# FFN weights freed of their mean, the first quad's q and k laid out by TensorE, the last y loaded in two parts, and new slots: a causal attention and FFN kernel on one core

## What is computed

```
def ffn(x):        # base + correction, W is 256x256, V_r and C have rank 32
    return x @ W.T + b + (x @ V_r) @ C.T

x = x + 0.5 * ffn(layernorm(x))          # "ln1"
q, k, v = split(layernorm(x) @ W_attn)   # "ln2"
s = q @ k.T / 4, causal
a = (s*s + 1 if s > 0 else 1 - s/100) / 1000
x = x + (a @ v) @ W_proj
x = x + 0.5 * ffn(layernorm(x))          # "ln3"
```

## Time and profile before

| | us |
|---|---|
| median of 3 runs | 1777.77 (1775.73 to 1783.82) |
| the profiled execution | 1776.91 |
| its span | 1775.2 |
| PE busy | 1620.3 (91%) |
| ACT, DVE, POOL busy | 1379.9, 1349.2, 1292.4 |
| first score starts at | 55.4 |
| last product of the attention ends at | 1734.45 |
| mean granted TensorE clock | 0.976 |

### The profile page before, as it was taken

How to read it: one execution, slowest core, us unless ns; L and a number is a source line. 1 busy time by engine, 2 the same in 40 slices (tenths; PEclk the granted TensorE clock), 3 DMA queues, 4 the chain that set the end, 5 groups by cost and what they waited for, 6 DMA issues and landing times.

```text
span 1775.2 us, 67710 instructions
## 1 busy us (share of the span) xinstructions
PE 1620.3 (91%) x27158; PEld 822.4 (46%) x27158; DVE 1349.2 (76%) x3229; ACT 1379.9 (78%) x2214; POOL 1292.4 (73%) x1455
## 2 busy tenths in 40 slices
PE   6787989999998999999998999999998999899994
PEld 3453444444445544444445544444455545344442
DVE  4767777878787787878887787887878677788881
ACT  2456768988887888888886888888887887788881
POOL 2566657777878896878878797877878787677662
PEclk9888999999999999999999999999999999999997
DMA  3653532432446443332436534243434535322211
GB/s 100 182 161 102 167 117 81 131 90 79 116 115 175 136 145 112 112 112 80 145 100 167 167 114 136 80 132 103 130 104 141 156 99 157 90 69 67 81 41 53
DMA packets 183222, 206.16 MB, mean 116 GB/s; under 512 B 27004, under 2 KB 156916, under 8 KB 181116
## 3 DMA queue, kind: packets, MB, share of 16 engines
q1 hardware_dynamic: 182908, 201.77, 39.2%
HBM read 123.65 MB, written 76.30 MB: 113 GB/s over the span
## 4 chain that ended last, share of the span: by engine, by line
PE 60%; DVE 15%; POOL 9%; ACT 8%; issue 5%; DMA 1%; SPq 1%; POOLq 0%; ACTq 0%; DVEq 0%
PE y_ps L1215 23%; PE score L1215 18%; PE bank L1215 16%; DVE rp L1148 9%; POOL rp L938 4%; ACT rp L1045 3%; PE bank L1241 3%; ACT rp L1065 2%; DVE lin L1154 2%; POOL z L900 2%; DVE bnst_ln L1173 1%; POOL rp L913 1%; PE bank L1280 1%; POOL lin L913 1%; ACT rp L1061 1%
## 5 line engine op out<-in xcount | busy, mean ns | idle before, releaser
L1148 DVE TENSOR_SCALAR rp<-score 128x512 f32<-128x512 f32 (+3 forms) x1728 | 973.1, 591 | 274.4 <-PE score L1215 272.5
L938 POOL TENSOR_TENSOR rp<-rp 128x1024 f32<-128x1024 f32 (+3 forms) x416 | 710.9, 1716 | 95.1 <-DVE rp L1148 82.5
L1215 PE MATMUL score<-qs,ks 96*32 96x512 bf16 (+3 forms) x10240 | 722.0, 352 | 51.8 <-DVE lin L1154 21.7
L1215 PE MATMUL y_ps<-rp,vt 128*16 128x512 f32 (+3 forms) x5120 | 599.5, 536 | 36.2 <-DVE lin L1154 12.2
L1045 ACT ACTIVATE rp<-score 128x512 f32<-128x512 f32 (+3 forms) x832 | 435.4, 561 | 203.8 <-PE score L1215 199.3
L1215 PEld LDWEIGHTS score<-qs,ks 96*32 96x32 bf16 x10240 | 299.1, 96 | 431.6 <-DVE rp L1148 161.2
L1061 ACT ACTIVATE rp<-rp,rise 128x1024 f32<-128x1024 f32 (+3 forms) x416 | 438.8, 1077 | 6.5 <-POOL rp L913 6.4
L913 POOL TENSOR_SCALAR_AFFINE_SELECT rp<-rp 128x256 f32<-128x256 f32 (+1 forms) x400 | 189.9, 475 | 262.0 <-ACT rp L1045 191.7
L1065 ACT ACTIVATE rp<-rp 128x2048 f32<-128x2048 f32 (+2 forms) x224 | 342.6, 1529 | 16.0 <-POOL rp L913 14.6
L1154 DVE SCALAR_TENSOR_TENSOR lin<-score,slope_mask 128x128 f32<-128x128 f32 x736 | 206.3, 280 | 0.0
L1215 PEld LDWEIGHTS y_ps<-rp,vt 128*16 128x16 f32 x5120 | 138.0, 96 | 133.6 <-issue 32.4
(11 more groups left out here) (80 smaller groups left out, 1293.6 us busy)
## 6 DMA issues: line engine op xcount, KB each, us to landing
ks<-part_scratch SPq DMA_DIRECT2D x648, 64.0 KB, 2.4
qs<-part_scratch SPq DMA_DIRECT2D x384, 64.0 KB, 2.3
part_scratch<-parts SPq DMA_DIRECT2D x14, 1536.0 KB, 5.9
vt<-v_scratch SPq DMA_DIRECT2D x103, 128.0 KB, 2.6
state_scratch<-st_new SPq DMA_DIRECT2D x16, 528.0 KB
x_sb<-in_L_attn_x_dram SPq DMA_DIRECT2D x16, 512.0 KB, 4.4
x_scratch<-x SPq DMA_DIRECT2D x16, 512.0 KB, 5.4
qT_scratch<-qkT SPq DMA_DIRECT2D x16, 512.0 KB, 3.3
```

The lines of the kernel that those rows point to most:

```text
L938: pool.tensor_tensor(half, half, half, ALU.mult).then_inc(squared["pool"], 1)
L1148: nc.vector.tensor_scalar(rp[T % RP_BUFS][:, 2 * u + v, off:CH], score[H % S_BUFS][:, v, off:CH], 0.0, RISE, ALU.max, ALU.add).then_inc(ra ...
L1215: return nc.tensor.matmul(*args, start=start, stop=stop, skip_group_check=True)
```

## The change

**The weights.** Two things are subtracted on DVE during the start: from each row of W (held in `w_in`) its mean over the 256 inputs, and from each row of V_r transposed its mean. A product with weights whose input mean is zero is the same for x and for x minus its mean. So for ln1 and ln3 PE transposes `x_sb` or `x2` itself, the statistics serve the scale alone, and DVE multiplies the product by `rstd` when it adds x, in two instructions of 256 elements per bank where one of 512 stood. L900 and L1107 stay for ln2 only. `z3` is gone; `z3T` is a tile of its own.

**The first quad.** `pick` is a matrix of zeros and ones. PE multiplies the split parts of the first chunk's q and k with columns of it (`spread`), which puts them on the 96 rows in `score`; ACT and DVE copy them to `qs` and `ks` (`lay_out`), at slots 13 and 17 behind the start of B. 12 loads fall away.

**The split.** Heads 0 to 7 (side 0) and 8 to 15 (side 1) have a `rest` and a semaphore each. In the first four chunks DVE splits side 0 and POOL side 1.

**The last y.** For the last two chunks the load of y is in two parts: what the first three quads wrote is loaded from DRAM ahead, and the last quad's y goes from `y_sb` to `y_c` directly in four DMAs.

**Slots.** `WHOLE`, all tables, `LENGTHS`, `HALVES_AFTER` and `LATE` have new numbers, and some DMAs of the start have other slots.

```diff
-WHOLE = [1, 3, 6, 10, 16, 17, 20, 23, 26, 28, 31, 33, 35, 38]
+WHOLE = [1, 3, 6, 10, 14, 17, 20, 23, 26, 28, 30, 33, 35, 39]
-A_FULL = {"z1T": (32, 35), "ffn": (38, 40), "z2T": (64, 64), "ln1": 9, "ln2": 48}
+A_FULL = {"z1T": (30, 31), "ffn": (37, 39), "z2T": (64, 64), "ln1": 21, "ln2": 48}
-HALVES_AFTER = (36, 33)
+HALVES_AFTER = (24, 33)
+            def load_c_before(c):
+                ...
+                sp.dma_start(y_c[:, 0, :], y_d[0:P, cols]).then_inc(c_loaded, 16)
+                sp.dma_start(y_c[0:QD, 1, :], y_d[P:P + QD, cols]).then_inc(c_loaded, 16)
+                sp.dma_start(x1c[:], x1_d[cols, :].rearrange("(i p) d -> p i d", p=P)).then_inc(c_loaded, 16)
+            def load_c_last(c):
+                w = VISIT[c // CPB, QUADS - 1, c % CPB]
+                sp.wait_ge(y_copied, w + 1)
+                for h in range(QH):
+                    sp.dma_start(y_c[QD + HD * h:QD + HD * h + HD, 1, :],
+                                 y_sb[w % 2][STRIP * h:STRIP * h + HD, :]).then_inc(c_loaded, 16)
-                    nc.vector.tensor_tensor(x1[:, 2 * i:2 * i + 2, :], two, x_sb[:, 2 * i:2 * i + 2, :], ALU.add).then_inc(done, 1)
+                        dve.wait_ge(rstd_done["ln1"], a + 1)
+                    for j in range(2):
+                        blk = 2 * i + j
+                        ins = nc.vector.scalar_tensor_tensor(x1[:, blk, :], two[:, j, :], rstd["ln1"][:, blk:blk + 1], x_sb[:, blk, :],
+                                                             ALU.mult, ALU.add)
+            nc.vector.tensor_reduce(w_mean[:], w_in[:], AX.X, ALU.add).then_inc(w_centred, 1)
+            ...
+            for k in range(KC):
+                nc.vector.tensor_scalar(w_in[:, k, :], w_in[:, k, :], w_mean[:, k:k + 1], None, ALU.add).then_inc(w_centred, 1)
+            ...
+            nc.vector.tensor_scalar(vrT[:], vrT[:], vr_mean[:, 0:1], None, ALU.add).then_inc(vr_centred, 1)
                 for b, i, step in split_at.get(s, ()):
-                    if b >= EARLY and step != 1:
+                    if step != 1 if b >= EARLY else i % KC:
                         split(pool, b, i, step)
+            def spread(which):
+                pe.wait_ge(pick_ready, 3)
+                pe.wait_ge(split_step[0], 3 * which + 3)
+                for u in range(QH):
+                    if which:
+                        pe.wait_ge(laid_out["dve" if u % 2 else "act"], u // 2 + 1)
+                    for j in range(0, len(PAIRS), 2):
+                        both = [PAIRS[j][which], PAIRS[j + 1][which]]
+                        for i, part in enumerate(sorted(set(both))):
+                            window = HD if both == [part, part] else 2 * HD if both[0] == part else 0
+                            ins = mm(score[u // 2][HD * j:HD * j + 2 * HD, u % 2, :], pick[:, u, window:window + 2 * HD],
+                                     parts[:, KC * which, part, :], start=i == 0, stop=i == len(set(both)) - 1)
+                    ins.then_inc(spread_out, 1)
```

More of the change, by code:

```diff
@@ L261, in finish @@
         for (kind, chunk), at in self.ln.items():
-            for step in range(BIAS + NB):
+            for step in range(NORM + NB):
                 self.steps.setdefault(at + step, []).append((kind, chunk, step))
@@ L353, with c_loads @@
 ORDER = order()
+BY_QUAD = (NCH - 2, NCH - 1)
+def c_loads(a):
+    return 2 * (a + 1) + sum(QH + 1 for c in BY_QUAD if c <= a)
 EARLY = CPB
@@ L407, in build @@
         parts = sb("parts", [P, 2 * KC, SPLITS, CH], BF16)
-        rest = sb("rest", [P, CH])
+        rest = [sb(f"rest{i}", [P, CH]) for i in range(KC)]
         st_new = sb("st_new", [QR, NB, HEADS * STRIP])
@@ L464, in build @@
         c_loaded = sem("c_loaded")
[L465 removed]
+        out_stored = [sem(f"out_stored{i}") for i in range(2)]
         xb_ready = sem("xb_ready")
@@ L688, in _ @@
                         put(x.empty_at + (7 if x.chunk else 2), "first st", x.chunk)
-                if (x.kind, x.i) == ("proj", 0):
+                if (x.kind, x.i) == ("proj", 0) and x.chunk in BY_QUAD:
+                    other_y = o.copy_slot[VISIT[x.chunk // CPB, QUADS - 2, x.chunk % CPB]]
+                    put(max(o.place["proj", x.chunk - 1, 1].empty_at, other_y + 8) + 1, "c before", x.chunk)
+                elif (x.kind, x.i) == ("proj", 0):
                     last_y = o.copy_slot[VISIT[x.chunk // CPB, QUADS - 1, x.chunk % CPB]] if x.chunk < NCH else o.again
@@ L738, in slot @@
                         b, = args
-                        sp.wait_ge(split_step, 12 * b + 12)
+                        for side in range(KC):
+                            sp.wait_ge(split_step[side], 6 * b + 6)
                         if b >= DIRECT:
@@ L832, in slot @@
                         load_c(*args)
+                    if what == "c before":
+                        load_c_before(*args)
+                    if what == "c last":
+                        load_c_last(*args)
                     if what == "out":
@@ L1129, in empty @@
                         dve.wait_ge(x2b_ready, a + 1)
-                    nc.vector.tensor_tensor(x2[a % 2][:, 2 * i:2 * i + 2, :], two, x2[a % 2][:, 2 * i:2 * i + 2, :], ALU.add).then_inc(done, 1)
+                        dve.wait_ge(rstd_done["ln3"], a + 1)
+                    for j in range(2):
+                        blk = 2 * i + j
+                        ins = nc.vector.scalar_tensor_tensor(x2[a % 2][:, blk, :], two[:, j, :], rstd["ln3"][:, blk:blk + 1],
+                                                             x2[a % 2][:, blk, :], ALU.mult, ALU.add)
+                    ins.then_inc(done, 1)
                 if kind == "state":
```

218 lines of the change are left out of this document (144 added, 74 removed).

## The result

The changed kernel takes 1714.37 us in the median of 4 runs (1713.6 to 1720.62); the kernel before took 1776.75 us beside it. The ratio is 0.965, 95% interval 0.961 to 0.969: 62 us less, where 30 were forecast, and outside the range (1731 to 1765).

A forecast was written before the change was run, and what follows sets the result against it. PE was taken to bound the middle (94% busy), a chain of single steps the end. Terms of -17.3 - 9 - 4 = -30.3 against 1776.9 gave 1746.6, with 0.9 for the median 1747.5, stated as 1747 us; range 1731 to 1765.

The forecast's parts named there:

- Term 1: The end, behind the attention's last product: direct y load, earlier transposes and full PE clock give -17.3 us; bound -11.9.
- Term 2: The middle, 215 us to the attention's last product: fewer PE waits for POOL and DVE, -9 us; bounds 0 and -30.
- the new `WHOLE` trades tiles of equal width: Middle: apart from diagonal tiles, the trade is equal; some -13 us for ACT, +3 for POOL, nothing for DVE.
- one loss of 3 us: Chunks 10 to 13: transposes one slot behind the DVE add they wait for, up to 1 us each, 3 in all.
- Of DVE's 43.4 I take 3: Middle: of 43.4 us of PE waits that DVE ends, 3 us go, as DVE's load falls by 1%.
- Term 3: The start and first chunks: centring, first quad by products, moved work and splits together give -4 us; bounds -12 and +6.
- I let these two cancel: First chunks, behind visit 4: DVE's relief by eight sides balances POOL's 24 added split instructions, 28 us.
- a sign of being wrong: First chunks: DVE's splits lasting over 3 us a side, with PE waiting behind them, would show the forecast wrong.
- The waits go as well: Rival, chance 0.08: all POOL waits, a quarter of DVE's and the best start are gained too, -17.3 - 30 - 8, 1722 us.
- POOL's 18.9 us: Middle: PE waits that POOL ends, 18.9 us (11.5 + 7.4); the forecast took half, 9, as gained.
- Only the end pays: Rival, chance 0.22: middle waits move from POOL to DVE and ACT, the start gives nothing; only -17.3, 1760.5 us.

The follow-up runs named there:

- e8: Changed kernel with the last two chunks' y loaded as before, stored to DRAM by quad and loaded whole behind the last store: 1724.39 us.
- e9: Changed kernel with the slot tables of the full and last chunks and `WHOLE` put back to those of before (ln1, ln3 starts excepted): 1729.41 us.
- e11: Changed kernel with POOL's normalising and its waits in the old places and DVE's 32 small shifts put back, all as unused work: 1744.48 us.
- e1: Changed kernel with the slot tables of the full and last chunks put back, ln1 and ln3 starts excepted, `WHOLE` staying new: 1737.4 us.
- e7: Changed kernel with the 32 small shift instructions of ln1 and ln3 put back on DVE as unused work: 1724.79 us.
- e5: Changed kernel with 96 unused POOL normalising instructions of ln1 and ln3 in the old slots, PE waiting for them, statistics moved back too: 1742.36 us.
- e4: Changed kernel with POOL's 128 normalising instructions put back as unused work in the bias's slots, nobody waiting for them: 1742.56 us.
- e12: Changed kernel with one unused POOL normalising and PE's wait for it put back at chunk 4's transposes, early chunks' statistics 5 slots sooner: 1725.53 us.
- e10: Changed kernel with the splits of q and k of chunks 0 to 3 all on DVE, as before: 1727.75 us.
- e13: Changed kernel with the undoings of e9, e11, e10 and e8 together: 1790.6 us.
- e6: Changed kernel with the unused normalising and waits of e5 and the old slots of e1 together, `WHOLE` staying new: 1775.11 us.

## Why the prediction was wrong

**Term 1, the end: right.** -17.3 forecast, -18.2 measured, each step within 0.3 us. e8 shows the shorter way: its projection begins 5.4 us later and takes 5.12 us, not 3.66.

**Term 2, the middle: the step that failed.** -9 forecast with -30 as bound; from the seventh copy to T it was -42. Three things were wrong in it.

- The tables were taken as sums of work ("the new `WHOLE` trades tiles of equal width"), and of the slots only one loss of 3 us was priced. They are worth 15 us (e9), and e11 gains 7 in the steady part with nearly the old work. What they change is which piece is late: with the old slots `y_ps<-DVE lin` and `bank<-DVE st_add` come back (e1), and DVE waits for POOL's bias, for which the prediction had no term.
- "Of DVE's 43.4 I take 3, since DVE's load there falls by 1%": the shifts alone give 10 (e7). 10 of 23.5 us came through, where PE was waiting for DVE anyway, as at 545.96 us. POOL's share depends on the place: 4 (e5) or 15 us (e4) in the steady part, and 9 in the late part (e4).
- A wait was priced at its length. One of 7.06 us gave 8.7 from copy 7 to copy 8 and 11.2 in the median (e12), since PE's products behind it ran slower for some 5 us. The other 3.9 us of that stretch's 12.7 are DVE's splits (e10), which the prediction had cancelled in its third term.

The late part (-11.7) is mostly POOL's relief: e4 loses 9.1 there, e1 and e9 2.3, e7 3.7. So POOL's and DVE's relief and the wait for `z` stood in this term, each too small; the worth of the slots and the slower products behind a wait did not.

**Term 3, the start: two errors that partly met.** Forecast -4. The first score came at 55.3, not 54, and the work put behind it shows in the fourth copy of y, at 129.8 us where it was at 125.7 before. "I let these two cancel", DVE's relief by eight sides and POOL's 28 us, was wrong: with all splits on DVE the kernel takes 13.4 us more (e10), for DVE and not POOL sets the pace there. POOL's `z` waits were counted at 3.8 and 7.4; in e5 three such waits, 16.4 us long, go with a loss of 22.6, its moved bias and statistics included. Against that stood losses that e13 leaves unexplained in part.

The rule from the page GPSIMD Engine Reference of the Trainium skill (section 1, Specifications), contention of GpSimd with VectorE's two-input and two-port instructions, would have made the splits on two engines slower. The trace bears it out as a stretch: undisturbed, a side's three steps on DVE take 0.68 + 0.43 + 0.69 = 1.8 us before, after and in e10, and every step of over 1 us lay beside an instruction of POOL. But POOL's squares and bias do most of it, which stand there anyway: a side takes 2.79 us in the mean with splits on POOL and 2.65 without (e10), and the cast is 2.00 at worst in both. POOL's own splits stretched two steps of DVE, 1.54 in place of 0.69. Three of the eight sides lasted over 3 us, which the prediction had named as a sign of being wrong, and yet the split on two engines was a gain.

**The rivals.** "The waits go as well" (1722) was the nearest: POOL's 18.9 us went but for 0.9, and of DVE's 43.4 there went 7.3. Its bound for the middle, -30, was still too near; it had 0.08, since DVE, behind most of the waits, was thought hardly relieved, and the tables were no part of it. "Only the end pays" (1760.5) came out in no run: e6 has the end's gain too, but loses it ahead of T and takes 1775.1.

## What to carry to other kernels

When a change comes with a new table of slots, price the table as a part of its own: look which piece of work each wait of the bottleneck engine ends at, and how many slots it stands late, not only how much work each engine has. For an engine that the bottleneck waits for often, its removed work counted here at a half or more (10 of 23.5 us in e7, 13 of 20 in e10), not at its share of the load; and a long wait of PE counted at 1.2 times its length (8.7 for 7.06, e12), since its products ran slower behind it. When an order of steps changes, as that of bias and transposes here, look who waits for the step that now comes later. Undoing parts one by one gives prices that don't add: the changes of e1 and e5 together cost 10 us more than their sum.
